# The last cross attention's top 32 on 50 full row tiles, its mean over heads by TensorE products

## The reference

```python
B, T, H, DH, K_TOP = 16, 100, 4, 32, 32
Q = (x_text @ Wq).reshape(B, T, H, DH)
K = (x_vision @ Wk).reshape(B, 1444, H, DH)
scores = einsum('bthd,bghd->bhtg', Q, K) / sqrt(DH)
scores = where(vision_mask[:, None, None, :], scores, -inf)
topv, topi = top_k(scores, K_TOP)
probs = softmax(topv)
attn = zeros_like(scores).at[bi, hi, ti, topi].set(probs)
attn_mean = attn.mean(axis=1)                 # over the 4 heads
c_t = einsum('btg,bgd->btd', attn_mean, x_vision @ Wv)
# c_t then scales and shifts the input and output of a state-space filter
```

## Time and profile before

| | us |
|---|---|
| median of 3 runs | 5116.3 |
| lowest and highest | 5106.44, 5136.1 |
| the profiled execution, from its first to its last instruction | 5139.5 |
| first MAX8 of the stage | starts at 3804.8 |
| last MATCH_REPLACE8 of the stage | ends at 4625.5 |
| VectorE goes on with c_t (L2491) | 4655.0 |

### The profile page before, as it was taken

The page is one execution under the profiler, slowest core; times in us unless marked ns, Lnnn a source line. Parts: engine busy times, 40 slices in busy tenths (PEclk is TensorE's granted clock), DMA queues, the critical chain, the costliest instruction groups (busy, mean ns, idle before and its releaser), DMA issues. The chain is left out here.

```text
span 5139.5 us, 86857 instructions
## 1 busy us (share of the span) xinstructions
PE 4115.3 (80%) x26550; PEld 2846.4 (55%) x26550; DVE 2994.6 (58%) x4577; ACT 2115.7 (41%) x3227; POOL 1733.6 (34%) x1171
## 2 busy tenths in 40 slices
PE   8899999999979988778789999994763434336699
PEld 4588888888867746534445555552432222223377
DVE  4344445444523444446545676656459999996433
ACT  3255555555522232124324555542235555551122
POOL 2266666666524232004310000000225555541033
PEclk8799999999969988799867999996876666667699
DMA  2000000000002203220022222210010101000011
GB/s 85 1 10 19 10 19 19 19 10 19 10 1 62 59 1 91 48 61 2 1 56 47 65 62 62 62 33 1 1 24 18 26 17 26 17 19 1 0 61 48
DMA packets 124607, 152.80 MB, mean 30 GB/s; under 512 B 86912, under 2 KB 110224, under 8 KB 124080
## 3 DMA queue, kind: packets, MB, share of 16 engines
q1 hardware_dynamic: 124208, 147.72, 11.5%
HBM read 109.43 MB, written 2.66 MB: 22 GB/s over the span
## 5 line engine op out<-in xcount | busy, mean ns | idle before, releaser
L989 POOL TENSOR_TENSOR pexp_lo<-arena,pexp_hi 128x800 fp32r<-128x800 f32 x384 | 635.7, 1655 | 443.2 <-POOLq L988 442.5
L2173 DVE TENSOR_REDUCE arena<-ps 100x1 f32<-100x482 f32 (+1 forms) x768 | 489.9, 657 | 266.8 <-DVEq L2160 256.5
L2053 DVE TENSOR_REDUCE arena<-ps 128x1 f32<-128x482 f32 (+3 forms) x624 | 392.9, 656 | 365.6 <-DVEq L2031 354.8
L1330 ACT ACTIVATE arena<-ps 128x800 f32<-128x800 f32 x384 | 322.3, 839 | 500.3 <-ACTq L1328 497.8
L2471 DVE MATCH_REPLACE8 arena<-arena 100x1444 f32<-100x1444 f32 x256 | 420.8, 1656 | 0.0
L1420 ACT ACTIVATE arena<-ps 128x800 f32<-128x800 f32 x384 | 315.5, 837 | 249.8 <-ACTq L1419 243.6
L3202 PE MATMUL ps<-kst,qs 96*100 96x482 f32 (+1 forms) x768 | 376.2, 492 | 43.0 <-PEq L3156 39.4
L935 POOL TENSOR_TENSOR max_diag<-w_const,arena 100x800 fp32r<-100x800 f32 x160 | 246.8, 1543 | 436.5 <-POOLq L933 436.5
L3331 PE MATMUL ps<-w_const,w_cross 100*128 100x100 f32 x192 | 43.2, 380 | 374.1 <-PEq L3328 374.1
L1331 ACT ACTIVATE pexp_hi<-ps 128x800 fp32r<-128x800 f32 x384 | 319.5, 832 | 0.0
L2573 DVE TENSOR_TENSOR arena<-ps,arena 128x400 f32<-128x400 f32 x256 | 147.1, 575 | 280.2 <-DVEq L2572 280.2
(11 more groups left out here) (393 smaller groups left out, 9621.0 us busy)
## 6 DMA issues: line engine op xcount, KB each, us to landing
ctxT<-in_ctxT SPq DMA_DIRECT2D x56, 541.5 KB
kst<-mid SPq DMA_DIRECT2D x128, 180.5 KB, 3.1
ctxk<-in_ctx SPq DMA_DIRECT2D x40, 528.0 KB
chunk<-in_ff_chunks SPq DMA_DIRECT2D x77, 193.0 KB, 2.4
arena<-gate_dram SPq DMA_DIRECT2D x64, 200.0 KB, 3.8
kst<-xn SPq DMA_DIRECT2D x64, 180.5 KB, 2.9
arena<-gate_dram SPq DMA_DIRECT2D x64, 100.0 KB, 2.6
arena<-in_ctxT SPq DMA_DIRECT2D x8, 541.5 KB
```

What stands on the lines that cost most here:

```text
L989: own(nc.gpsimd.tensor_tensor(pexp_lo[p % 3][:, :, :], pexp[p % 3], pexp_hi[p % 3][:, :, :], ALU.subtract))
L1330: nc.scalar.activation(pexp[p % 3], of, ACT.Exp, scale=scale).then_inc(s.pexp_ready, 1)
L2053: peak = nc.vector.tensor_reduce(mparts[0:at.stop - at.start, m, c:c + 1], bank(k, z - a, at.stop - at.start), AX.X, ALU.max)
L2173: peak = nc.vector.tensor_reduce(mparts2[:, h, c:c + 1], bank(k, z - a, S), AX.X, ALU.max)
```

## The change

- Rows are tiled flat over heads and tokens. Of the 400 rows of a batch 384 fill three tiles of 128 partitions, and the 16 left over (the last 16 tokens of head 3) of eight batches make one more tile. That is 48 + 2 = 50 tiles, 25 pairs (`PERIODS`) in place of 32. The order of tiles is the list `PAIRS_OF_ROWS`.
- The scores of a tile of leftovers need the contexts of eight batches. They are loaded in advance into room lent by `w_cross` and by the weight chunks of the feed-forward part (`lent_keys`), the first six behind the last weights before the stage, the others in the stage. Its products use 32 columns of the weight side for two batches each, four groups on different columns, 24 products.
- The head-mean, the scaling and the transposing are TensorE products: for each 128 keys, `kept` (keys as weights, 128 rows x 128 keys) times a 0/1 matrix `token_cols` with rows scaled by 1/denominator, three products of 100 columns and one of 16 columns for the leftovers, all summed in PSUM. The 64 scalings of 1444 columns become 50 small ones of 100 or 128 columns, and the additions on GpSimd, the transposes and the wait for them are gone.
- Two PSUM banks, 6 and 7, are used in turn (`side_bank`).
- `film_sides(n)` puts the mean of a batch into the period after the one that holds its last tile: periods 2, 4, 6, 7, 9, 10, 12, 13, 15, 16, 18, 19, 21, 22 and 24, and behind the last pair for batch 15.
- All masks are turned to 0 or -1e30 once, at the start of the kernel, and stored in DRAM; the stage loads a ready row. The folding of Wq and Wk goes ahead of the layernorm, the copy to `mid` behind the release of TensorE and ScalarE. The loops of the stage are written out.

The core of the diff:

```diff
+    PAIRS_OF_ROWS = [[("left", 0, 0), ("full", 0, 0)], [("full", 0, 1), ("full", 0, 2)],
+                     [("left", 1, 0), ("full", 1, 0)], [("full", 1, 1), ("full", 1, 2)]]
+    for b in range(2, B, 2):
+        PAIRS_OF_ROWS += [[("full", b, 0), ("full", b, 1)], [("full", b, 2), ("full", b + 1, 0)],
+                          [("full", b + 1, 1), ("full", b + 1, 2)]]
+    def film_sides(n):
+        return ([("mean", b) for b in range(B) if LAST_OF[b] + 1 == n]
+                + [("queries", b) for b in range(1, B) if max(FIRST_OF[b] - 2, 0) == n])
...
@@ SP, after the first loads
+        sp.dma_start(mask_raw, dram["ctx_mask"]).then_inc(s.text_mask_loaded, 16)
+        sp.wait_ge(s.mask_ready, 1)
+        sp.sem_inc(s.mask_ready, -1)
+        sp.dma_start(mask_dram, mask_add).then_inc(s.scratch_stored, 16)
...
@@ SP, film_block
+            own_keys(0)
+            own_keys(1)
+            sp.wait_ge(s.w_cross_free, 1)
+            for b in range(2, 7):
+                lent_keys(b)
...
+            for b in range(2, B):
+                own_keys(b)
+                rows(b)
...
@@ POOL
-                    own(nc.gpsimd.tensor_tensor(expd[k], expd[k], left[k], ALU.subtract))
-                        own(nc.gpsimd.tensor_tensor(attn[par], attn[par], expd[k], ALU.add))
+                    own(nc.gpsimd.tensor_tensor(kept_of(*tile), kept_of(*tile), left[k], ALU.subtract))
...
@@ ACT, scale
-                    to = attn[par] if k == 0 else expd[k]
-                    nc.scalar.activation(to, expd[k], ACT.Copy, scale=den[:, k:k + 1]).then_inc(s.scaled_ready, 1)
+                    to = by_row[b] if kind == "left" else by_token[b % 2][:, m, :]
+                    of = W("const", "ident") if kind == "left" else W("const", "token_cols")[:, S * m:S * m + S]
+                    nc.scalar.activation(to, of, ACT.Copy, scale=den[:, k:k + 1]).then_inc(s.scaled_ready, 1)
...
@@ ACT, order
+            for n in range(PERIODS):
+                exponents(n)
+                if n > 0:
+                    scale(n - 1)
+                if n + 1 < PERIODS:
+                    scores(n + 1)
+                sides(n)
+                sums(n)
...
@@ PE, mean
-                        ins = nc.tensor.transpose(bank(6, S, r, t % 4 * S), attn[par][:, 128 * t:128 * t + r], ident[0:S, 0:S])
+                        mm(bank(k, S, r, at), kept[b % 2][0][:, keys], by_token[b % 2][:, 0, :], start=True, stop=False,
+                           skip_group_check=True)
+                        mm(bank(k, LEFT, r, at + S - LEFT), kept_left[j][:, keys], by_row[j][:, LEFT * row:LEFT * row + LEFT],
+                           start=False, stop=False, skip_group_check=True)
+                        for m in range(1, FULL_TILES):
+                            ins = mm(bank(k, S, r, at), kept[b % 2][m][:, keys], by_token[b % 2][:, m, :], start=False,
+                                     stop=m == FULL_TILES - 1, skip_group_check=True)
...
@@ PE, order
+            for n in range(PERIODS):
+                if n + 1 < PERIODS:
+                    scores(n + 1)
+                sides(n)
+            sides(PERIODS)
```

More of the change, by code:

```diff
@@ L853, in film_block @@
             sp.dma_start(text_mask.bitcast(U8), dram["text_mask"].to_broadcast([128, T])).then_inc(s.text_mask_loaded, 16)
[L854 to L858, removed]
+            sp.wait_ge(s.fold_read, 1)
+            sp.sem_inc(s.fold_read, -1)
+            for b in (8, 10, 12, 14, 9):
+                lent_keys(b)
+            rows(0)
+            rows(1)
+            sp.wait_ge(s.fold_read, 1)
+            sp.sem_inc(s.fold_read, -1)
+            for b in (11, 13, 15):
+                lent_keys(b)
+            for b in range(2, B):
+                own_keys(b)
+                rows(b)
             feed_forward(3)
@@ L1469, in scores, with exponents @@
                     act.sem_inc(s.scores_there, 1)
-            def exponents(half):
-                for i in range(2):
-                    k = 2 * half + i
+                    if (kind, b) == ("left", 0):
+                        act.sem_inc(s.fold_read, 1)
+                    if (kind, m) == ("full", FULL_TILES - 1):
+                        act.sem_inc(ctx_free[b % 2], 1)
+            def exponents(n):
+                for i, tile in enumerate(PAIRS_OF_ROWS[n]):
+                    k = 2 * (n % 2) + i
                     act.wait_ge(s.low_ready, 1)
@@ L1476, in exponents, with sums @@
                     own(nc.scalar.activation(low[:, k:k + 1], tops[:, k, 0:1], ACT.Copy, scale=-1.0))
-                    own(nc.scalar.activation(expd[k], scores_sb[i], ACT.Exp, bias=low[:, k:k + 1]))
-            def sums(half):
-                for k in (2 * half, 2 * half + 1):
+                    own(nc.scalar.activation(kept_of(*tile), scores_sb[i], ACT.Exp, bias=low[:, k:k + 1]))
+            def sums(n):
+                ks = (2 * (n % 2), 2 * (n % 2) + 1)
+                for k in ks:
                     act.wait_ge(s.taken_ready, 1)
@@ L2477, in film_block @@
             dve.sem_inc(s.scores_sb_free, 2)
-            pair(0, first=True)
-            pair(1)
-            with dve.Fori(0, B - 1) as i:
-                pair(0)
-                pair(1)
+            for n in range(PERIODS):
+                pair(n)
             finished(1)
             dve.sem_inc(s.taken_ready, 1)
-            scales(1)
+            scales((PERIODS - 1) % 2)
             dve.wait_ge(s.ct_ready, 1)
@@ L3291, in film_block @@
         def film_block(layernorm, feed_forward):
+            for h in range(TH):
+                ins = mm(bank(4, C, 128, C * h), W("tk", "wq")[:, h * 128:h * 128 + 128], W("tk", "wk")[:, h * C:h * C + C],
+                         start=True, stop=True)
+            ins.then_inc(s.folded, 1)
             layernorm(x)
@@ L3344, in mean, with sides @@
                 pe.sem_inc(s.uv_ready, -1)
-                pe.wait_ge(s.proj_free, 1)
-                pe.sem_inc(s.proj_free, -1)
-                mm(bank(6, S), W("tk", "wv"), uv, start=True, stop=True).then_inc(s.proj_full, 1)
-            def batch(b, par, first=False):
-                if not first:
-                    mean(1 - par)
-                queries(b + 1)
-                for h in range(TH):
-                    scores(h, 1 - par)
-            queries(0)
-            for h in range(TH):
-                scores(h, 0)
-            batch(0, 0, first=True)
-            with pe.Fori(0, B // 2 - 1) as i:
-                batch(2 * i + 1, 1)
-                batch(2 * i + 2, 0)
-            mean(0)
-            mean(1)
+                k = side_bank()
+                mm(bank(k, S), W("tk", "wv"), uv, start=True, stop=True).then_inc(s.proj_full, 1)
+            def sides(n):
+                for kind, b in film_sides(n):
+                    (mean if kind == "mean" else queries)(b)
+            left_queries()
+            queries(0)
+            pe.wait_ge(s.row_ones, 1)
+            pe.sem_inc(s.row_ones, -1)
+            pe.wait_ge(s.qv_ready, 1)
+            pe.sem_inc(s.qv_ready, -1)
+            scores(0)
+            for n in range(PERIODS):
+                if n + 1 < PERIODS:
+                    scores(n + 1)
+                sides(n)
+            sides(PERIODS)
+            pe.wait_ge(s.proj_free, 2)
+            pe.sem_inc(s.proj_free, -1)
             layernorm(mid)
```

321 lines of the change are left out of this document (186 added, 135 removed).

## The result

| | before | after |
|---|---|---|
| median of 20 runs each, us | 5132.12 | 5104.57 |
| lowest and highest | 5106.44, 5187.52 | 5070.82, 5170.18 |
| ratio, 95% interval | | 0.9931 [0.9906, 0.9957] |
| profiled execution, span | 5139.5 | 5102.4 |
| first MAX8 to the end of the last replacement | 820.7 | 760.4 |

The kernel gains 0.7% (22 to 48 us, some 35), where I had forecast 2.3% (116 us). The ratio leaves out three executions that lie over 1.5% above the fastest of their kernel; the medians hold them. In the profiles the stage itself gives 60.3 + 10.2 - 22.8 = 47.7 us.

A forecast was written before the change was run, and what follows sets the result against it. VectorE was taken as the bound, 25.62 us per pair of tiles. Fewer pairs (-179.3), start (-5.5), waits (2 x 5.0 and 6 x (5.0 + 0.8)) and end (+24.1) gave -115.9 us, from 5116.3 to 5000; range 4920 to 5085.

The forecast's parts named there:

- Part 1: Row tiles: VectorE's instructions cost the same with 128 rows, so 25 pairs in place of 32 save 179.3 us.
- rival E: Row tiles: VectorE's scans grow with rows, 820 us as now; +10 to +20 us, 5130; chance 0.03.
- Part 3: Head-mean on TensorE: 96 records spaced by weight loads; the mean lasts 28.3 us at 1.2 GHz, 16.8 at 2.4.
- Rival D: Mean's products: 128-column weight loads don't hide behind products, 14.7 us more per mean; 5304 us; chance 0.07.
- Who waits: VectorE waits for ScalarE's sums behind the mean: 5.0 us (slow) or none after first means, 12.3 or 0.8 after second.
- the end: From the last replacement to the mask product: 53.6 us against 29.5 before, +24.1 us.
- the one called least certain: TensorE's clock: first means run at 1.2 GHz without rising, second means, 1 to 2.5 us behind scores, at 2.4 GHz.
- the fast D: Length of a mean on TensorE at 2.4 GHz: 16.8 us.
- rival C: Gap between scores and second mean drops the clock; all means at 1.2 GHz; -47 us, 5069; 0.26 including mixtures.
- the mechanism of B: The forecast itself: first means at 1.2 GHz, second at 2.4 GHz; -115.9 us, 5000; chance 0.46.
- rival A: All means at 2.4 GHz, no wait remains, the end about as now; -186 us, 4930; chance 0.14.
- Start: Ahead of the first maximum: copy and folds leave the path, leftover scores take 12 turns, 7.5 us; -5.5 us.

The follow-up runs named there:

- e7: The changed kernel with five unused filling products of 400 columns ahead of each of the six second means only; ratio 0.9803 to the kernel before.
- e3: The changed kernel with TensorE's idle gaps ahead of the means filled by products nobody uses; ratio 0.9655 to the kernel before.
- e9: The changed kernel with the leftover product moving 100 columns, the first 16 wanted, the surplus overwritten or unread; full output; ratio 0.9621 to the kernel before.
- e2: The changed kernel without the 16-column leftover product per 128 keys, so the output is incomplete; ratio 0.9586 to the kernel before.
- e8: The changed kernel with the leftover product moving 100 columns of other rows in place of its 16, so its sums are wrong; ratio 0.9635 to the kernel before.
- e4: The changed kernel with ScalarE's sums moved ahead of the mean's third group of copies; ratio 0.9643 to the kernel before.
- e11: The changed kernel with the exact 100-column leftover product, sums ahead of the mean's third copies, diagonals a period early, no filling; ratio 0.9625 to the kernel before.

## Why the prediction was wrong

**Held.** Part 1: 1648 ns a scan, periods of 25.6 us; rival E (scans that grow with the rows) is out. Part 3, the mean: 0.213 us per record at 1.2 GHz and 0.112 at 2.4, with 16 moving columns as with 100; to the first `ctxk` product 20.2 + 1.55 = 21.75 forecast, 21.9 measured, and 10.6 + 1.55 against 12.2 in e7. Its whole length D was 27.4 us for batch 14 (4551.08 to 4578.46) and 28.3 for batch 15 (4589.72 to 4618.06), forecast 28.3. Rival D is out: the weight loads hide. Who waits: D - 23.3 = 5.0 forecast, 6.0 measured (mean of eight, by the periods); D - 16.0 = 12.3 forecast for the slow second mean, 11.8 measured (mean of six). In the rows:

```profile
4564.52 1.65 DVE L2542 MATCH_REPLACE8 arena<-arena 128x1444 f32<-128x1444 f32 x1
4579.60 0.17 DVE L2510 RECIPROCAL arena<-arena 128x2 f32<-128x2 f32 x1 [13.43 <-DVEq L2509]
4618.50 1.83 DVE L2559 TENSOR_TENSOR arena<-arena 128x1600 f32<-128x1600 f32 x1 [38.74 <-DVEq L2558]
```

which answer: the end took 52.3 us, +22.8, against the forecast's 53.6 and +24.1. The first waits are 1.0 us longer for a term that the forecast left out. It let the sums end 1.0 us behind the mean; in seven of the eight periods ScalarE copies the next batch's queries (L1524) between the two, and they end 1.8 to 2.6 us behind it:

```profile
4105.51 0.25 ACT L1601 ACTIVATE arena<-ps 128x100 f32<-128x100 f32 x1 [1.32 <-ACTq L1518]
4106.84 0.50 ACT L1524 ACTIVATE arena<-ps 96x400 f32<-96x400 f32 x1 [1.08 <-ACTq L1518]
4107.67 0.32 ACT L1568 ACTIVATE arena<-arena 128x32 f32<-128x32 f32 x1 [0.33 <-ACTq L1567]
```

**The step that failed** is the one called least certain: "A second mean follows the scores of the next pair after 1 to 2.5 us: I take 2.4 GHz, as that stream held it". Six second means were priced at the fast D, and all six ran at 1.2 GHz but for two starts. Three came behind a gap of 2.7 to 3.4 us, longer than assumed; two of them began at 2.4 GHz and lost it within some 1.2 us, the third was at 1.2 from the start. The other three (4022.14, 4305.63, 4401.02) came right behind the scores, without a gap, but those scores were themselves slow, behind a gap of 2.9 to 3.0 us of their own: 5.15 us for six records against 2.66.

```profile
4016.90 5.15 PE L3426 MATMUL ps<-ctxT,arena 97*128 97x482 f32 x6 [2.91 <-PEq L3424]
4022.14 0.72 PE L3441 MATMUL ps<-arena,w_cross 128*128 128x100 f32 x2
```

So the gap of rival C is only half of it; the other half is a stream that does not rise again. Nor was the assumed gap a safe one: in e3 a mean lost the clock behind 1.6 us. Six waits of 11.8 in place of 0.8 are 66 us. With the rest of the sum (8 x 1.0 more on the first waits, 4.7 less at the start, 1.3 less at the end) that makes -115.9 + 66 + 8 - 4.7 - 1.3 = -47.9, and the profile has -47.7. The mechanism is that of case C, which had 0.26. That its -47 is met so closely is luck: against its sum the second waits are 3 us less, the first 8 more and the ends 6 less. e7 shows the counter-case: with the gap filled the mechanism of B appears, 57 us of stage below after.

**The reason under it was wrong too.** For the first means I wrote "no rise, since its weights leave more time between columns than the 24 products that didn't lift the clock". The result was right, the cause not: e9 has the same weights at the same distance, and every mean rises to 2.4 GHz or holds it. What kept the clock from rising is the one product in four that moves 16 columns and takes a full record's time (e2 without it and e8 and e9 with it widened rise). It does not bring the clock down by itself, as e3, e4 and e7 show, where the same stream holds 2.4 GHz. I had priced that product by its time alone ("no cheaper"), which was right for its time and missed its effect on the other 66 records of the mean. Hence rival A (0.14) was refused for the wrong reason: three changed lines bring about nearly its time, 0.9621. Forecast for A was -186 us; e9's stage with its start, 10.0 us shorter than before's, is 678.3 - 850.2 - 10.0 = -182.

The Trainium skill (TensorE: Matmul & The Clock Gate, Part 1) says that sustained matmul activity releases the clock; the trace agrees for e8 and e9, and disagrees for after, where 18 us without an idle moment stayed at 0.50; the measurement decides. A record in flight all the time was not enough here, and the busy column of a stretch doesn't show the difference.

**Start.** -10.2 us against -5.5: in this profile the last TENSOR_SCALAR ahead of the stage starts at 3780.47 and the first MAX8 at 3805.77, behind the copy to `mid`, which now lies beside TensorE's work as forecast.

```profile
3796.19 0.99 DVE L2496 COPY mid<-xn 128x1600 f32<-128x1600 f32 x1 [0.42 <-DVEq L1700]
3805.77 1.67 DVE L2519 MAX8 arena<-arena 128x8 f32<-128x1444 f32 x1 [8.58 <-DVEq L2518]
```

The 12 turns of products for the leftovers' scores took 5.0 us (L3403, 3798.65 to 3803.65) against 7.5 forecast. The 25.3 us of this start were 25.2 to 29.6 in the eleven kernels of the experiments, which have the same code there, so a part of the 4.7 us is this profile's luck.

**The range.** 4920 to 5085 held case C (5069) but no spread of the kernel itself. From the forecast of 5000 to the median of 5104.6 it is 104.6 us. Some 68 are the stage (-47.7 in place of -115.9), and 16 the base: the median of before was 5116.3 in three runs and is 5132.1 in 20. The remaining 20 lie between the stage's 47.7 and the 27.6 by which the medians differ; no cause is shown for them. In the two profiles the stage is 47.7 us shorter and the span 37.1, the difference being 11.2 us lost ahead of the stage, in code that the change touches only in the mask work at the kernel's start, and 0.6 gained behind it. The 11.2 are within what the same code varies by (below).

## What to carry to other kernels

Where a short product stands in a stream that is bound by its weight loads, widen it to the others' columns and let the surplus fall where it is overwritten: here it cost no time at either clock and let the whole stream rise to 2.4 GHz. When a stage's bound engine waits on a chain through TensorE, price the chain at both clock levels and find which one it gets by trying, since the profile's busy share doesn't tell. Count every operation between the links of such a chain. Compare single profiles by the stage, not by their spans, where another stage's clock varies from run to run.

## What the runs showed of the hardware

A fp32 product of 16 columns with 128 weight columns costs as much as one of 100 (0.213 us per record at 1.2 GHz, 0.112 at 2.4), and widening it made the kernel about 3% faster (0.9931 to 0.9621). Products with no use at all, put ahead of the stream, did it too: 0.9655 in e3. The stream with the 16-column products did not rise in 14 means of 16, yet held 2.4 GHz to the end in the 11 of e3 that began less than 0.5 us behind other products; the two of e3 behind gaps of 1.6 and 2.2 us began at 2.4 GHz and lost it.

Identical code ahead of the stage took up to 56 us more or less: the first MAX8 came at 3781.2 in e11 and at 3837.0 in e9. Some 40 of the 56 us arise in the third cross attention, between 2620 and 2830, where the DVE timelines of the two part, and most of the rest near 3300. Stretches of it, in after, e9 and e11:

```profile
2600.00:2850.00 250.00, 235.95 (x1963) 142.76 (x1964) 142.42 (x240) 97.11 (x132) 14.54 (x12) 0.69 0.23 50
```

```profile
2600.00:2850.00 250.00, 235.58 (x1813) 144.44 (x1813) 130.32 (x220) 91.42 (x126) 15.76 (x13) 0.63 0.21 47
```

```profile
2600.00:2850.00 250.00, 229.09 (x2269) 137.58 (x2268) 159.45 (x272) 112.17 (x155) 16.94 (x14) 0.87 0.26 57
```

TensorE is busy over 90% of it each time, at a granted clock of 0.63 to 0.87, and gets through 1813 to 2269 records. So the clock that this one stage is granted makes most of the spread between these profiles. What decides it wasn't tried.
